# A gated linear attention and mixture-of-experts block on one core: running sum of the gates ahead of the output products, routing weights by ScalarE and GpSimd, one expert loaded per step

## The reference, cut to what is computed

```python
h = layernorm(x) * (1 + ca) + sa                  # ca, sa, ga, ... from silu(c) @ wmod
q, k, v = h @ Wq, h @ Wk, h @ Wv                  # 16 heads of 16
g = log_sigmoid(h @ Wgk1 @ Wgk2 + bgk2) / 16
state = state * exp(g_t) + v_t k_t^T              # per token and head; out_t = state q_t
x = x + ga * ((layernorm(out) * gamma + beta) * silu(h @ Wg)) @ Wout
h = layernorm(x) * (1 + cb) + sb
scores = h @ Wr + br                              # top 2 of 8
w = softmax(scores of the chosen two)             # the routing weights
x = x + gb * sum_e w_e * (gelu(h @ W1[e] + b1[e]) @ W2[e] + b2[e])
```

## Time and profile before

| | |
|---|---|
| median of 3 runs | 1006.52 us (1006.07 to 1009.92) |
| the profiled execution | 1005.15 us |
| its span, first to last instruction | 1003.4 us |
| PE busy | 905.2 us, 90% |
| DVE busy | 735.7 us, 73% |
| ACT busy | 482.6 us, 48% |
| POOL busy | 421.1 us, 42% |
| first half | up to about 500 us, one step each 13.8 us once it runs evenly |

### The profile page before, as it was taken

The page is one execution under the profiler, slowest core; times in us unless marked ns, Lnnn a source line. Parts: engine busy times, 40 slices in busy tenths (PEclk is TensorE's granted clock), DMA queues, the critical chain, the costliest instruction groups (busy, mean ns, idle before and its releaser), DMA issues.

```text
span 1003.4 us, 27282 instructions
## 1 busy us (share of the span) xinstructions
PE 905.2 (90%) x7353; PEld 746.6 (74%) x7354; DVE 735.7 (73%) x1908; ACT 482.6 (48%) x1552; POOL 421.1 (42%) x448
## 2 busy tenths in 40 slices
PE   6769999999999999997699898999999989999895
PEld 4446556566565665564589898999989989999895
DVE  3469999999999999998666666666666675666663
ACT  4255566655666556663234343434343434344431
POOL 4226655556555565555213232323323333233232
PEclk9889999999999999999799999999999999999998
DMA  7934334343343443343282222222212222122121
GB/s 232 374 125 144 108 122 139 131 142 116 114 142 129 140 137 104 131 138 122 95 283 42 34 43 32 43 32 43 38 32 40 40 33 43 32 43 40 32 39 24
DMA packets 84395, 97.22 MB, mean 97 GB/s; under 512 B 6705, under 2 KB 79618, under 8 KB 84226
## 3 DMA queue, kind: packets, MB, share of 16 engines
q1 hardware_dynamic: 71040, 78.74, 23.8%
q0 software_dynamic: 12864, 17.83, 10.4%
q10 hardware_dynamic: 450, 0.17, 0.1%
HBM read 38.91 MB, written 57.80 MB: 96 GB/s over the span
## 4 chain that ended last, share of the span: by engine, by line
PE 58%; DVE 16%; issue 10%; DVEq 7%; ACT 4%; SPq 2%; DMA 1%; ACTq 0%; POOL 0%; POOLq 0%
PE p_a L1127 19%; PE p_cum L1127 8%; PE p_qk L1127 7%; PE p_z L1127 7%; PE p_vg L1127 7%; PE p_o L1127 6%; DVE w_hi L877 4%; SPq L455 2%; DVE host_s_r L1111 1%; DVE x L952 1%; DMA host_x<-in_L_attn_x_dram 1%; PE p_tr L1327 1%; DVEq L1076 1%; PE p_o L1147 1%; DVEq L1075 1%
## 5 line engine op out<-in xcount | busy, mean ns | idle before, releaser
L654 POOL DMA_INDIRECT out_dram<-x,tok x68 | 163.5, 2404 | 336.3 <-DVE x L1104 309.7
L681 ACT ACTIVATE h2T<-p_tr,mods 128x128 f32<-128x128 f32 x200 | 80.6, 453 | 335.4 <-PE p_tr L1327 280.0
L1127 PE MATMUL p_a<-w_hi_r,host_s_r 128*128 x544 | 146.3, 300 | 12.1 <-DVE host_s_r L1111 12.1
L1127 PE MATMUL p_a<-w_r,host_s_r 128*128 x544 | 140.6, 290 | 0.0
L599 POOL TENSOR_TENSOR w<-qkT_both,own_half 128x512 f32<-128x512 f32 x64 | 65.1, 1035 | 177.2 <-ACT qkT_both L762 161.4
L1127 PEld LDWEIGHTS p_a<-w_hi_r,host_s_r 128*128 128x128 f32 x544 | 102.1, 188 | 14.7 <-issue 14.2
L1081 DVE COPY host_x<-w 128x1024 f32 x68 | 47.3, 695 | 89.4 <-issue 52.0
L1127 PEld LDWEIGHTS p_a<-w_r,host_s_r 128*128 128x128 f32 x544 | 102.4, 188 | 0.0
L877 DVE TENSOR_TENSOR w_hi<-p_a,upto 128x512 f32<-128x512 f32 x128 | 84.4, 680 | 6.3 <-PE p_a L1127 6.3
L634 POOL DMA_INDIRECT expert_rows<-rows,pos x64 | 64.1, 1002 | 50.9 <-POOL rows L631 22.5
L1127 PE MATMUL p_a<-w,qkT_both 64*128 64x512 f32 x256 | 75.0, 663 | 3.2 <-DVE mods L983 3.2
(11 more groups left out here) (214 smaller groups left out, 2147.0 us busy)
## 6 DMA issues: line engine op xcount, KB each, us to landing
expert_rows<-pad_rows SPq DMA_DIRECT2D x32, 1088.0 KB, 4.7
w<-in_L_ffn_W_dram SPq DMA_DIRECT2D x16, 1024.0 KB, 13.1
ln_host<-expert_rows SPq DMA_DIRECT2D x68, 136.0 KB, 2.1
host_x<-in_L_attn_x_dram SPq DMA_DIRECT2D x63, 128.0 KB, 2.1
out_dram<-x SPq DMA_DIRECT2D x32, 128.0 KB, 1.7
out_dram<-x,tok POOLq DMA_INDIRECT x68, 4.7
w<-in_L_wmod_dram SPq DMA_DIRECT2D x2, 512.0 KB, 5.4
b_all<-in_L_ffn_b_dram SPq DMA_DIRECT2D x1, 1024.0 KB, 4.3
```

Of the source, the lines that this page charges most:

```text
L654: nc.gpsimd.indirect_dma_start(out=out, out_offset=bass.IndirectOffsetOnAxis(ap=tok[u][:, 0:1], axis=0), in_=y_out[u][:], in_offset=None, ...
L681: last = A.activation(dst[:, j, :], src[:, j * P:(j + 1) * P], ACT.Identity, scale=mods[:, which + 2 + j:which + 3 + j], bias=mods[:, whic ...
L1127: return nc.tensor.matmul(dst, lhsT, rhs, start=start, stop=stop, skip_group_check=True)
```

## The change

Four things move. On PE the running sum (`p_cum`) goes ahead of the wait for x1 and of the first output products. The routing weights leave DVE: ACT makes them at the end of its step with four instructions (exp of the gap, log(1+e), exp(-l), exp(gap-l)), and POOL lays them out by expert with two, a product over 128x16 and a sum over 128x8, ahead of its two indirect DMAs. DVE gets two waits more, for weights that were read and gates that were placed. The experts are loaded one per step, in steps 0, 1, 2, 3 and 30, at the end of SP's step, behind the store of x1. In DVE's step -1 the copy of the late modulation moves ahead of `vn`.

```diff
--- before.py
+++ after.py
@@ -206,12 +206,14 @@
         top = sb("top", [P, 8])
         top_i = sb("top_i", [P, 8], U32)
         top_f = sb("top_f", [P, TOP])
-        hot = [sb(f"hot{j}", [P, E]) for j in range(TOP)]
+        hots = sb("hots", [P, TOP, E])
+        hot = [hots[:, j] for j in range(TOP)]
         chosen = sb("chosen", [P, E], BF16)
         gap = sb("gap", [P, 1])
         gap_e = sb("gap_e", [P, 1])
-        wt = sb("wt", [P, 3])
-        wt_a = sb("wt_a", [P, E])
+        gap_l = sb("gap_l", [P, 1])
+        wt = sb("wt", [P, TOP])
+        wt_hot = sb("wt_hot", [P, TOP, E])
         base = sb("base", [P, E])
         slot = sb("slot", [P, E])
         pick = [sb(f"pick{j}", [P, E]) for j in range(TOP)]
@@ -341,7 +343,10 @@
         h2T_ready = sem("h2T_ready")
         score_ready = sem("score_ready")
         gap_ready = sem("gap_ready")
-        gap_exp = sem("gap_exp")
+        weights_ready = sem("weights_ready")
+        wt_hot_ready = sem("wt_hot_ready")
+        gates_placed = sem("gates_placed")
+        act_w = sem("act_w")
         chosen_ready = sem("chosen_ready")
         rank_ready = sem("rank_ready")
         ranks_taken = sem("ranks_taken")
@@ -486,6 +491,8 @@
                 load(w2[:, e * KF * D:(e + 1) * KF * D].rearrange("p (j n) -> p j n", j=KF),
                      W2[e].rearrange("(j p) n -> p j n", p=P), sm)
 
+            expert_at = {0: 0, 1: 1, 2: 2, 3: 3, NC - 2: 4}
+
             def step(s, u, front, back, finish, route):
                 v = 1 - u
                 if back and not (isinstance(s, int) and s + 2 >= NC):
@@ -506,8 +513,8 @@
 
                     sp.wait_ge(gates_ready, 1)
                     load(b2_all[:], b2.rearrange("(a e) d -> a (e d)", a=1).to_broadcast([P, E * D]), b2_loaded)
-                    for e in range(E - LATE):
-                        expert(e, experts_loaded)
+                if isinstance(s, int) and s in expert_at:
+                    expert(expert_at[s], experts_loaded)
 
             walk(sp, step)
 
@@ -629,7 +636,14 @@
 
                     wait_apart(pool, (xn2_ready, r + 1))
                     nc.gpsimd.tensor_copy(rows[u][:, ID:ID + 1], ids[:, bass.ds(r, 1)]).then_inc(id_ready, 1)
-                    wait_apart(pool, (id_ready, r + 1), (pos_ready, r + 1))
+                    pool.wait_ge(chosen_ready, r + 1)
+                    pool.wait_ge(weights_ready, r + 1)
+                    nc.gpsimd.tensor_tensor(wt_hot[:], hots[:], wt[:].unsqueeze(2).to_broadcast([P, TOP, E]),
+                                            ALU.mult).then_inc(wt_hot_ready, 1)
+                    pool.wait_ge(wt_hot_ready, r + 1)
+                    nc.gpsimd.tensor_tensor(rows[u][:, D:D + E], wt_hot[:, 0], wt_hot[:, 1],
+                                            ALU.add).then_inc(gates_placed, 1)
+                    wait_apart(pool, (id_ready, r + 1), (gates_placed, r + 1), (pos_ready, r + 1))
                     for j in range(TOP):
                         nc.gpsimd.indirect_dma_start(
                             out=scratch, out_offset=bass.IndirectOffsetOnAxis(ap=pos[u][:, j:j + 1], axis=0),
@@ -750,9 +764,6 @@
                     order.then(A.activation(ez[:], abs_z[:], ACT.Exp, scale=-1.0))
                     after(act_e, g_ready, f)
                     A.activation(lz[:], ez[:], ACT.Ln, bias=1.0).then_inc(log1p_ready, 1)
-                if route:
-                    act_e.wait_ge(gap_ready, s - 1)
-                    A.activation(gap_e[:], gap[:], ACT.Exp).then_inc(gap_exp, 1)
                 if front:
                     act_e.wait_ge(log_gate_ready, f + 1)
                     A.activation(silu[:], silu[:], ACT.Exp).then_inc(sigmoid_ready, 1)
@@ -782,6 +793,15 @@
                     act_e.wait_ge(o_ready, s + 1)
                     after(act_e, ot_ready, s)
                     A.copy(oT[:], p_o[:, 0:D]).then_inc(oT_taken, 1)
+                if route:
+
+                    act_e.wait_ge(gap_ready, s - 1)
+                    weight.begin(s - 2)
+                    weight.then(A.activation(gap_e[:], gap[:], ACT.Exp))
+                    after(act_e, gates_placed, s - 2)
+                    weight.then(A.activation(gap_l[:], gap_e[:], ACT.Ln, bias=1.0))
+                    A.activation(wt[:, 0:1], gap_l[:], ACT.Exp, scale=-1.0)
+                    A.activation(wt[:, 1:2], gap_l[:], ACT.Exp, scale=-1.0, bias=gap[:, 0:1]).then_inc(weights_ready, 1)
 
             walk(act_e, step)
             A.preload_act_table_set("gelu_apprx_tanh_and_others")
@@ -919,11 +939,13 @@
                     wait_apart(dve, (score_taken, r + 1))
                     ro.then(V.max(top[:], score[:]), apart=True)
                     ro.then(V.max_index(top_i[:], top[:], score[:]))
+                    after(dve, weights_ready, r)
                     V.tensor_tensor(gap[:], top[:, 1:2], top[:, 0:1], ALU.subtract).then_inc(gap_ready, 1)
                     ro.then(V.tensor_copy(top_f[:], top_i[:, 0:TOP]))
-                    ro.mark(V.tensor_scalar(hot[0][:], iota_e[:], top_f[:, 0:1], None, ALU.is_equal))
-                    ro.then(V.tensor_scalar(hot[1][:], iota_e[:], top_f[:, 1:2], None, ALU.is_equal))
-                    V.tensor_tensor(chosen[:], hot[0][:], hot[1][:], ALU.add).then_inc(chosen_ready, 1)
+                    after(dve, gates_placed, r)
+                    ro.mark(V.tensor_scalar(hot[0], iota_e[:], top_f[:, 0:1], None, ALU.is_equal))
+                    ro.then(V.tensor_scalar(hot[1], iota_e[:], top_f[:, 1:2], None, ALU.is_equal))
+                    V.tensor_tensor(chosen[:], hot[0], hot[1], ALU.add).then_inc(chosen_ready, 1)
                 if front:
 
                     dve.wait_ge(gate_log1p_ready, f + 1)
@@ -956,31 +978,19 @@
                 if finish:
                     dve.wait_ge(x1_ready, d + 1)
                     yo.mark(V.bn_stats(st_1[:], x1[v][:]))
-                if route:
-
-                    dve.wait_ge(gap_exp, r + 1)
-                    ro.then(V.tensor_scalar(wt[:, 0:1], gap_e[:], 1.0, None, ALU.add))
-                    ro.mark(V.reciprocal(wt[:, 1:2], wt[:, 0:1]))
-                if finish:
                     yo.sync(apart=True)
                     V.bn_aggr(mv_1[:, 0:2], st_1[:]).then_inc(x1_stats, 1)
-                if route:
-                    ro.sync()
-                    ro.mark(V.tensor_tensor(wt[:, 2:3], gap_e[:], wt[:, 1:2], ALU.mult))
-                    ro.then(V.tensor_scalar(wt_a[:], hot[0][:], wt[:, 1:2], None, ALU.mult))
-                    V.scalar_tensor_tensor(out=rows[u][:, D:D + E], in0=hot[1][:], scalar=wt[:, 2:3],
-                                           in1=wt_a[:], op0=ALU.mult, op1=ALU.add)
-                if front:
-
-                    dve.wait_ge(e_ready, f + 1)
-                    after(dve, u_ready, f - 1)
-                    V.tensor_tensor(vn[v], p_vg[:, 0:D].rearrange("p (h d) -> p h d", d=HD),
-                                    e_neg[:].rearrange("p (h d) -> p h d", d=HD), ALU.mult).then_inc(vn_ready, 1)
                 if isinstance(s, int) and s < 0:
                     dve.wait_ge(late_mods_ready, 1)
                     V.tensor_copy(b1_col[:], p_a[0][:, 0:E * KF])
                     setup.then(V.tensor_copy(mods[:, 4:8], p_a[0][:, E * KF:E * KF + 4]))
                     V.tensor_scalar(mods[:, 6:8], mods[:, 6:8], 1.0, None, ALU.add).then_inc(mods_taken, 1)
+                if front:
+
+                    dve.wait_ge(e_ready, f + 1)
+                    after(dve, u_ready, f - 1)
+                    V.tensor_tensor(vn[v], p_vg[:, 0:D].rearrange("p (h d) -> p h d", d=HD),
+                                    e_neg[:].rearrange("p (h d) -> p h d", d=HD), ALU.mult).then_inc(vn_ready, 1)
                 if isinstance(s, int) and s == 0:
                     dve.wait_ge(gates_copied, 1)
                     limit_gate(ga)
@@ -1264,6 +1274,12 @@
                     last.then_inc(y_ready, 1)
                 if nextx:
                     transpose_x(s + 2, u, s - 1)
+                if front:
+                    pe.wait_ge(g_ready, f + 1)
+                    after(pe, e_ready, f)
+                    for n, sums in enumerate((upto_half, ones)):
+                        last = mm(p_cum[:, n * D:(n + 1) * D], sums[:], g_log[:], True, True)
+                    last.then_inc(cum_ready, 1)
                 if back:
                     after(pe, x1_ready, s)
                     after(pe, state_ready, s)
@@ -1271,12 +1287,6 @@
                     if isinstance(s, int) and s == 0:
                         pe.wait_ge(gates_copied, 1)
                     output_of_block(0)
-                if front:
-                    pe.wait_ge(g_ready, f + 1)
-                    after(pe, e_ready, f)
-                    for n, sums in enumerate((upto_half, ones)):
-                        last = mm(p_cum[:, n * D:(n + 1) * D], sums[:], g_log[:], True, True)
-                    last.then_inc(cum_ready, 1)
```

(7 more changed lines are left out.)

9 lines of the change are left out of this document (7 added, 2 removed).

## The result

The changed kernel takes 993.26 us in the median of 4 runs (993.04 to 995.62). The kernel before took 1007.39 beside it. The ratio is 0.9866, 95% interval 0.9851 to 0.9881: faster by 1.3%, outside the 0.5% bound. The forecast was 989, range 980 to 1002. The profiled execution took 993.04 us, its span is 991.3; before it was 1005.15 and 1003.4, so 12.1 us went.

A forecast was written before the change was run, and what follows sets the result against it. The prediction took a ring in the first half, ACT, POOL's chain, cast, DVE, as the bound. Loop 9.8, start 7.8 and end 0.2 gave 17.8 off 1005.15, 987.3 profiled, 989 us median; range 980 to 1002.

The forecast's parts named there:

- Start, won: Step 1: x no longer queued behind ten expert transfers, 8.8 us, plus 1.4 from the clock; 10.2 us (8.8 to 10.5).
- Start, given back: Steps 1 to 3: x lands late behind an expert on SP, 0.8 us three times; 2.4 us lost.
- Rival 4: Start: a single expert takes 13.1 us to land, x late by 6 us three times; about 1005 us; chance 0.06.
- The loop: Steps 5 to 30: 13 pairs of steps, each gaining 0.95 less 0.2 for DVE's new waits; 9.8 us.
- Where the gain goes: Even steps: cast 0.75 us earlier, hT ahead of the state product; branch step's hT behind it, ending 0.2 earlier.
- rival 2: Loop: POOL's next product takes the port before DVE, cast stays behind the state product, gain 0; 998.5 us; chance 0.26.
- Rival 1: Loop: both kinds of step get ahead of the state product, 0.65 x 26 = 16.9 us; 982 us; chance 0.19.
- The ring through POOL: Even step: ACT to q, POOL's chain, cast, DVE and back to ACT close the ring.
- The port: DVE and POOL: a DVE instruction on SBUF operands stands until POOL's running one is through; cast ended 316.36, product 316.33.
- The new work: End of step: ACT's 0.9 us and POOL's two products hide in waits, costing nothing; DVE's new waits 0.1 a step.
- rival 3: Loop: POOL's new products take the port ahead of hT, 29 x 0.5 = 14.5 us lost; 1013 us; chance 0.07.
- The end: End of first half: five instructions leave DVE's last chain, but PE stood only 0.18 us for it; 0.2 us won.

The follow-up runs named there:

- e3: The kernel before with only the experts' part of the change, one expert per step: 1007.22 us, ratio 0.9999.
- e4: The changed kernel with the experts' part undone, the five experts all in step 0 again: 992.12 us, ratio 0.9862.
- e1: The kernel before with only the running sum moved ahead of the output products on PE: 1005.92 us, ratio 0.9989.
- e2: The kernel before with only the routing weights moved from DVE to ACT and POOL: 1006.22 us, ratio 0.9993.
- e6: The changed kernel with one unused 128x256 product (0.72 us) added on POOL between decay and the pair's product: 992.66 us, ratio 0.9848.
- e12: e9 with POOL's `b_ln` moved behind the state product: 990.37 us, ratio 0.9829.
- e10: The changed kernel with one unused 128x1024 product added on POOL between decay and the pair's product: 1050.96 us, ratio 1.0439.
- e9: The changed kernel with four unused 128x256 products added on POOL between decay and the pair's product: 1019.53 us, ratio 1.0093.
- e5: The changed kernel with experts 1 to 4 issued behind their step's load of the next x: 979.41 us, ratio 0.9730.

## Why the prediction was right, and where not

**Start, won.** Right: 10.2 forecast, 10.6 measured, the wait of 8.79 us gone and the granted clock at 1.00 over 55 to 60. That the two agree to 0.4 us is luck, for this point differs by more than that between executions (it gained 8.3 us in e3).

**Start, given back.** Mis-sized, the one large error: 2.4 forecast, 10.3 measured. The issue came where it was put (x1 + 0.8). The time for an expert and the x behind it was taken as 6.5 to 7.6 us, from the burst's rate and a lone transfer. It was 9.7 to 9.9. The rate alone was not the error: the engines moved 0.28 MB per us over the first of these stretches and 0.32 over the other two, where 0.34 was taken. They moved 2.8 to 3.1 MB, though, where 2.2 were counted. The forecast put the residual and the 1.1 MB of padding rows at nothing, as due later; they were issued before x had landed (the padding rows 3.7 to 5.3 us after the expert). That the surplus is theirs is likely but wasn't tried. DVE's waits sum to 9.2 us instead of 2.4, and the clock comes on top. The forecast counted it for the one wait of 8.79 us and not for the small ones, and behind two of the three it fell (2.08 and 1.66 us instead of 1.13 for the scores). "The granted clock at 1.0 from there" was wrong for these. The experts' edit was put at 7.8 us; e3 and e4 measured it at nothing. Rival 4 had the mechanism (x late each time), with twice the lateness.

**The loop.** Mechanism right, size near: 9.8 forecast, 12.85 measured. The step without the branch gained 0.73 (forecast 0.75), the branch step 0.21 (0.2), both without the 0.1 us a step that the forecast took off for DVE's two new waits. Two things make up nearly all of the rest: that 0.1 us isn't to be seen, which is 2.6 us over 26 steps, and the first pair behind the start gained 0.2 more than the others (13.18 and 13.59 against 13.90 and 14.01). `vn` came 0.63 earlier and not 0.47, mostly because the first exponential begins 1.84 us after x1; the forecast had put it at 1.96.

**The two edits pay only together.** Right: e1 0.9989, e2 0.9993, both of them with `vn` at 3.40, and e4 has the whole gain.

**Where the gain goes.** In the step without the branch it was as written: cast with the pair's product, hT ahead of the state product. In the branch step the 0.2 came about in another way, and that its size fits is luck. The picks were to run ahead of the pair's product and hT to stand for the state product. Instead a pick stands for the pair's product and the cast for the state product, as before, 0.2 us earlier after x1 (5.64 against 5.84 us at the cast's end). POOL's own chain lies that much earlier: its q starts 0.17 us ahead of x1, and 0.05 behind it before. The margin at `b_ln` that the forecast called 0.1 us decides between the two ways. In the step without the branch the norm starts 0.25 us before `b_ln` ends and passes (0.40 us); in the branch step it starts 0.10 us before and falls into the decay products (0.62 us). For that half of the steps the order is the one of rival 2, though not its zero. Rival 1, hT ahead of the state product in both, did not come.

**The ring through POOL.** The reading that POOL's chain closes the ring fell in e6: 0.7 us more in the chain cost 0.1 us a step, and in e12 2.8 us more cost nothing. What costs is the remainder of the product that DVE meets, as far as it moves the end of hT.

**The port.** The Trainium skill's page SBUF — State Buffer, section Who interferes with whom, says that whichever of the two is issued first blocks the other for the whole instruction, and that `tensor_scalar` and `cast` take both of the shared ports in their fast modes, while `tensor_tensor` takes only the one for reading. e10 agrees (2.17 us for an instruction of 2.37). The forecast's own instance of the rule for two inputs in SBUF was a cast, which has one and belongs to the other case; L969 in e1, a `tensor_tensor` with two, stood 0.73 us and fits as well. The page's section says nothing of who comes next when several are queued. e9's 4.71 us are beyond it. It was the norm, a `tensor_scalar`, that was kept out; that this is the reason wasn't tried.

**The new work.** Hidden, as forecast: ACT's four instructions take 0.9 us and end before its next input is there (8.8/15 = 0.6 us of waiting left, 26.3/15 = 1.75 before). POOL's two products of 0.21 and 0.20 to 0.26 us lie behind the state product, and hT beside them takes 0.47 us, not over 0.6, so rival 3 did not come.

**The end.** Forecast 0.2 won. DVE's last tables came 13.2 us earlier, but the warm-up products of PE took 10.58 us instead of 9.42, and the first tile gained 11.6. Why they took longer wasn't followed up.

**In sum** two terms erred in opposite directions. The start was put 7.8 - 0.3 = 7.5 us too high, the loop 3 too low, and the end 1.3 too high with all that follows the loop. For the profiled execution 987.3 was forecast and 993.04 measured, 5.7 us off; for the median 989 and 993.26. That the total came within 5 us is in part luck, since the loop's error cancels a third of the others. It says less than e4 and e5 do.

## What to carry to other kernels

When an edit takes work from an engine that waits anyway, look for the second wait of the same length: either edit alone is worth about 0.1% here (0.2% by the intervals), both 1.4%. Put a large load that is spread over steps behind the small load that the next step needs. An estimate of when the small one lands should look at what is issued behind it too: here the engines moved 2.8 to 3.1 MB where 2.2 were counted. On POOL, cut long SBUF products near DVE's short SBUF instructions: the same 1024 elements per partition cost 58 us in one instruction, and in four pieces none once `b_ln` was out of the way. Ask for each such DVE instruction which product it meets, and which instruction's end the length of the step follows.

## What the runs showed of the hardware

- DVE instructions of 1 to 8 elements per partition stand for the rest of POOL's running product: 0.65 us beside one of 0.72, 2.17 us beside one of 2.37. In nearly all steps DVE then goes ahead of the products that are queued. How late in a product DVE starts matters: in the changed kernel a norm that starts 0.25 us before the end of `b_ln` takes 0.40 us, one that starts 0.10 us before it takes 0.62.
- Not always: in every fourth step of e9 a norm that began 0.30 us after the start of a 0.72 us product stood 4.71 us, past seven more. Norms that began 0.52 to 0.55 us after it, in the same kernel, took 0.40. With that product elsewhere and POOL busy 86 of 100 us (e12), it did not happen in any even step. What decides the handing over is open.
- A load of 0.1 MB issued behind 2 MB was there 9.7 to 9.9 us after the first issue. Only a store of 0.1 MB was issued shortly ahead of them, but 1.2 MB more behind them before x was there, and the engines moved 2.8 to 3.1 MB in that time.
- Two waits in which PE sat idle 3.60 and 3.20 us were followed by a granted clock of 0.50 (0.76 and 0.88 over the 14 us around them), and four products took 2.08 and 1.66 us that take 1.13 at 1.00. A wait in which PE sat idle 1.96 us left the clock at 1.00.
